# GpSimd adds the two states of a group before TensorE transposes their sum

## The reference

```
h = da * h + dbu              # da = exp(dt * A), dbu = dt * B * u
y = einsum('bdn,bn->bd', h, c)
y = (y + u * D) * silu(z);  out = y @ W_out
```

## Time and profile before

| | |
|---|---|
| Median of 3 runs | 1932.57 (1929.4 to 1938.46) |
| Profiled execution, its own time | 1930.86 |
| Its span, first to last instruction | 1928.9 |
| PE (TensorE matmul) busy | 1582.0 (82%) |
| DVE (VectorE) busy | 1511.5 (78%) |
| ACT (ScalarE) busy | 1004.7 (52%) |
| POOL (GpSimd) busy | 829.6 (43%) |
| Mean granted TensorE clock | 0.88 of full speed |

### The profile page before, as it was taken

The page is one execution under the profiler, slowest core; times in us unless marked ns, Lnnn a source line. Parts: engine busy times, 40 slices in busy tenths (PEclk is TensorE's granted clock), DMA queues, the critical chain, the costliest instruction groups (busy, mean ns, idle before and its releaser), DMA issues. The chain is left out here.

```text
span 1928.9 us, 16561 instructions
## 1 busy us (share of the span) xinstructions
PE 1582.0 (82%) x5776; PEld 834.9 (43%) x5776; DVE 1511.5 (78%) x1622; ACT 1004.7 (52%) x1609; POOL 829.6 (43%) x443
## 2 busy tenths in 40 slices
PE   6767877788888779988788879988798988886975
PEld 2445334443456335543355335453355434552433
DVE  4896789957996889968998789969899689963242
ACT  4542755346663755537563655637554565633522
POOL 0764265515553265515554166524555155630000
PEclk9767888797899889997999879997999879997987
DMA  4000000000000000000000000000000000000000
GB/s 155 1 1 11 13 0 1 11 13 0 1 1 11 13 11 1 1 23 0 11 0 11 12 11 0 0 22 1 11 0 11 12 0 11 0 11 0 11 0 22
DMA packets 18058, 20.51 MB, mean 11 GB/s; under 512 B 1361, under 2 KB 16977, under 8 KB 18017
## 3 DMA queue, kind: packets, MB, share of 16 engines
q1 hardware_dynamic: 18016, 19.98, 3.2%
HBM read 15.79 MB, written 4.19 MB: 10 GB/s over the span
## 5 line engine op out<-in xcount | busy, mean ns | idle before, releaser
L419 POOL TENSOR_TENSOR reg_a<-reg_a,cb 128x1024 f32<-128x1024 f32 x256 | 603.5, 2358 | 476.3 <-DVE reg_a L1116 476.3
L1116 DVE TENSOR_TENSOR_SCAN reg_a<-reg_a,pb 128x1024 f32<-128x1024 f32 x256 | 584.2, 2282 | 30.4 <-ACT reg_a L884 19.9
L884 ACT ACTIVATE reg_a<-dt,neg_a 128x511 f32<-128x511 f32 x512 | 336.8, 709 | 46.7 <-DVE reg_a L1116 46.5
L1106 DVE TENSOR_TENSOR pb<-pb,dtu 128x1024 f32<-128x1024 f32 x256 | 309.8, 1210 | 65.4 <-PE pb L617 53.4
L638 PE MATMUL py<-ident,reg_a 128*128 128x128 f32 x2048 | 304.4, 298 | 22.8 <-POOL reg_a L419 22.8
L638 PEld LDWEIGHTS py<-ident,reg_a 128*128 128x128 f32 x2048 | 273.3, 156 | 76.1 <-POOL reg_a L419 26.0
L617 PE MATMUL pb<-bcs,sel 96*128 96x512 bf16 x512 | 180.2, 440 | 95.1 <-DVE reg_a L1116 87.9
L519 PE MATMUL px<-hT,whh 128*128 128x512 f32 x384 | 203.7, 656 | 0.0
L786 ACT ACTIVATE xs<-px,half_b 128x512 f32<-128x512 f32 x96 | 66.0, 688 | 151.4 <-PE px L523 150.6
L617 PEld LDWEIGHTS pb<-bcs,sel 96*128 96x128 bf16 x512 | 38.2, 103 | 245.0 <-DVE reg_a L1116 146.9
L596 PE MATMUL pc<-x2T,w_fc 128*128 128x512 f32 x224 | 110.0, 615 | 20.9 <-DVE reg_y L1130 13.5
(11 more groups left out here) (179 smaller groups left out, 2318.4 us busy)
## 6 DMA issues: line engine op xcount, KB each, us to landing
xin<-x_in SPq DMA_DIRECT2D x9, 512.0 KB, 3.6
xs<-x_in SPq DMA_DIRECT2D x8, 512.0 KB, 3.4
x_out<-reg_m SPq DMA_DIRECT2D x8, 512.0 KB, 3.0
w_in<-w_inT_in SPq DMA_DIRECT2D x1, 1024.0 KB, 6.4
w_fc<-w_fcT_in SPq DMA_DIRECT2D x1, 1024.0 KB, 10.7
w_pr<-w_prT_in SPq DMA_DIRECT2D x1, 1024.0 KB, 13.0
xs<-wihT_in SPq DMA_DIRECT2D x1, 768.0 KB, 8.6
whh<-whhT_in SPq DMA_DIRECT2D x1, 768.0 KB, 8.7
```

What stands on the lines that cost most here:

```text
L419: pool.tensor_tensor(h[:, g % HR], h[:, g % HR], cb[:, 2 * q:2 * q + 2], ALU.mult).then_inc(s["hc_done"], 1)
L884: ins = act.activation(d_a[:, g % 2, j, 1:], dt[:, c, 1:], ACT.Exp, scale=neg_a[:, c * NS + n + j:c * NS + n + j + 1])
L1106: dve.tensor_tensor(pb[:, b:b + 2, :], pb[:, b:b + 2, :], dtu[:, c:c + 1, :].to_broadcast([P, 2, L]), ALU.mult).then_inc(s["mul_done"], 1)
L1116: dve.tensor_tensor_scan(h2[:, g % HR], d_a2[:, g % 2], pb[:, b:b + 2, :].rearrange("p a t -> p (a t)"), 0.0, ALU.mult, ALU.add).then_inc( ...
```

## The change

GpSimd gets a second instruction per group. After the multiply with C it waits for its own completion and adds state 1 of the slot to state 0, in place, 128x512; the new semaphore `hp_done` signals it. TensorE waits for `hp_done` in place of `hc_done` and transposes only the four blocks of state 0, which now hold the sum of both. The accumulation in `py` runs over the 8 groups of a chunk.

```diff
@@ -81,7 +81,7 @@
-cb_full cb_ready bcb_full da_ready mul_done scan_done hc_done hsum_done ypost_done yz_done
+cb_full cb_ready bcb_full da_ready mul_done scan_done hc_done hp_done hsum_done ypost_done yz_done
@@ -417,6 +417,8 @@
                         pool.tensor_tensor(h[:, g % HR], h[:, g % HR], cb[:, 2 * q:2 * q + 2], ALU.mult).then_inc(s["hc_done"], 1)
+                        pool.wait_ge(s["hc_done"], g + 1)
+                        pool.tensor_tensor(h[:, g % HR, 0], h[:, g % HR, 0], h[:, g % HR, 1], ALU.add).then_inc(s["hp_done"], 1)
                     if mamba and chunk_end(g) is not None:
@@ -629,14 +631,13 @@
                 c, q = g // PAIRS, g % PAIRS
-                pe.wait_ge(s["hc_done"], g + 1)
+                pe.wait_ge(s["hp_done"], g + 1)
                 if q == 0 and c:
                     pe.wait_ge(s["yt_ready"], c)
-                for j in range(2):
-                    for i2 in range(TT):
-                        cols_ = slice(i2 * P, (i2 + 1) * P)
-                        mm = pe.matmul(py[:, cols_], h[:, g % HR, j, cols_], ident[:], is_transpose=True,
-                                       start=(q == 0 and j == 0 and i2 == 0), stop=(q == PAIRS - 1 and j == 1), skip_group_check=True)
+                for i2 in range(TT):
+                    cols_ = slice(i2 * P, (i2 + 1) * P)
+                    mm = pe.matmul(py[:, cols_], h[:, g % HR, 0, cols_], ident[:], is_transpose=True,
+                                   start=(q == 0 and i2 == 0), stop=(q == PAIRS - 1), skip_group_check=True)
                 mm.then_inc(s["hsum_done"], 1)
```

## The result

The changed kernel takes 2006.72 us (median of 4 runs, 2002.22 to 2010.7) against 1931.92 for the kernel before: ratio 1.0388, 95% interval 1.0369 to 1.0406. It is slower by 75 us where 34 were forecast; the stated range ended at 1986. The sign was right, the size off by a factor of two.

What follows compares the result with a forecast made beforehand. VectorE was taken as the bound, with 15 us idle per batch. Seven full batches at +3.5 (3.6 + 3.6 + 2.4 + 0.9 - 7.0) gave +24.5, with pass 0 +34: 1965 us from 1930.9, range 1938 to 1986.

Steps and rivals of the forecast that it cites:

- The collisions on VectorE: Full passes: adds delay VectorE's SBUF-to-SBUF instructions L1014/L1016, L1027/L1029 and L1019 by 3.6, 3.6 and 2.4 us per pass.
- Taking turns on the port: VectorE's SBUF-to-SBUF instructions and GpSimd's alternate, each waiting for the other's to finish; an add costs the second instruction 1.2 us.
- rival 3: GpSimd keeps the port through multiply and add, or TensorE is granted less clock: 4 us more per batch, 1993; chance 0.15.
- The gains on TensorE's side: Full passes: fewer transposes shorten VectorE's idle time behind TensorE by 2.2, 3.0 and 1.75 us in three rounds, together 7.0.
- The prediction's own sign: Full batch: VectorE's idle time for the broadcasts of B (L617) falls from 6.8 us to under 3.
- Its part on the clock: Whole kernel: granted clock may shift either way, +-20 us at the extreme; taken as zero.
- Pass 0: First batch: GpSimd becomes the bound at 3.66 us per group; +9.5 us, bounds +6 and +13.
- the drought: Pass 0, merge of the weights: GpSimd runs out of work while TensorE is away from the groups; 1.5 us.
- The end of a pass: After a batch's last scan nothing covers GpSimd: +1.32 us for the add, -0.43 for fewer transposes, +0.9.
- Rival 1: TensorE was the hidden bound and L1016 and L1029 escape collisions: full batch gains 6.1 us, 1897; chance 0.12.
- Rival 2: A wash: collisions about 5 us per batch in place of 9.6, about 1933; chance 0.15.
- rival 4: The add doesn't bind in pass 0: 9.5 us less, 1955; chance counted within the forecast's 0.58.

Runs made afterwards that it cites:

- The run with memsets: Changed kernel with three waiting GpSimd memsets of a scratch tile, together about 1.3 us, in place of each add; state 1 left out of y: 1964.7 us, ratio 1.0154.
- a choice by groups: Changed kernel with add and four transposes only in ten groups of passes 1 to 7, eight transposes elsewhere: 1910.4 us, ratio 0.9894 to the kernel before.
- the kernel with twenty adds: Changed kernel with add and four transposes only in 20 of 32 groups of passes 1 to 7, none in pass 0: 1934.3 us, ratio 1.0009.

## Why the prediction was wrong in size

- *The collisions on VectorE* (3.6 + 3.6 + 2.4 = 9.6 per full pass, 67): the mechanism was right, the sum right partly by luck. VectorE's busy time rose by 70.1. But the two pairs brought 17 and 20 in place of 25 each: the second instruction waits 0.95 (medians 1.64 and 2.17) in place of 1.2, and six of the 24 L1017 and three of the 24 L1030 met no add (three rounds of each lie in the pass without a Mamba block). L1020 brought 20 for 17. L937, which was set to be hidden, made up for the shortfall with 11 us. The run with memsets adds what the prediction had only for L1019: half of the 70 comes from a late GpSimd, not from the add's own reading.
- *Taking turns on the port*: right: the exclusive port pair of the Trainium skill's "SBUF — State Buffer" ("SBUF: two separate sides") holds in the timeline of L1015 and L1017, and only instructions with SBUF operands alone were held here. So rival 3 (GpSimd keeps the port) is out in its first form: L1028 is unchanged (2945 to 2939 ns), L1009 no longer than before (median 1.50 in both). The other half of rival 3, less clock, is what happened; its sign, a clock in the groups under 0.92, came (0.88).
- *The gains on TensorE's side* (7.0 per pass, 49): this is the step that failed. With the ends of the passes and pass 0 the prediction's terms for the removed transposes come to 53. Measured: 24 with the transposes removed only in the stretches for which the 49 were counted, 17 with all removed, 9.5 with all removed beside the add. So there are three shortfalls. First, even in those stretches a full pass gains 3.7, not 7.0: VectorE's waits for L617 and L790 shrink by 5.1 (in pass 4), but L1019 and L1050 then meet GpSimd, and the output projection comes 1.6 later by the clock. Pass 1, for which the same 7.0 was counted, gains nothing there. Second, the prediction took removals elsewhere for neutral. In the full passes they are; in pass 1 they cost 5.7, where TensorE comes to a stretch that binds at half clock. Third, beside the add another 8 go, which no run takes apart. The prediction's own sign, VectorE's wait for L617 falling from 6.8 to under 3 in a full pass, did not come (4.0 in pass 4 of the changed kernel, and 56.0 for 53.4 over the run). Its part on the clock took it for luck with two signs and set it to zero. Wherever transposes were removed in all groups or in those where nobody waits, the clock fell (0.846, 0.837, 0.861 for 0.880); removed only where VectorE waits, it stayed (0.883). No run changes the clock and nothing else, so what it costs is read from equal matmuls that took longer.
- *Pass 0* (+9.5): +12.6, and 13 to 15 by the run without the add there. GpSimd is the bound as forecast, its last transposes came at 184.35 for 182 (180.6 and the drought); the difference is the merge of the weights at half clock, with a VectorE wait of 6.92 for 4.36 and a drought of 3.5 for 1.5. But the pace of 3.66 held only for a few groups: after the merge the scans stand at 3.50, since the merge had emptied GpSimd's queue, and GpSimd fell behind again by 0.16 a group until the end.
- *The end of a pass* (+0.9): about +1.3, since four transposes at half clock take what eight took: nothing came off the 1.3 of the add.
- *The sum.* By the run with the add and eight transposes, the add costs 84, where the prediction's terms for it come to 87 (67 on VectorE, 7 x 1.3 at the ends, 10.5 in pass 0); the removed transposes give back 9.5, where they come to 53. So 87 - 53 = 34 was forecast and 84 - 9.5 = 75 measured: nearly the whole error is the gain on TensorE's side.
- Rival 1 (TensorE the hidden bound, the collisions missing) is refuted twice: the collisions came, and not over 24 us were to be had on TensorE's side. Rival 2 (collisions of 5 per batch) and rival 4 (the add hidden in pass 0) are out by the 70 and the 12.6.

## What to carry to other kernels

Removed work counts only where others wait for it, and not in full even there: behind the wait that shrinks stands the next one, here GpSimd's instructions and TensorE's clock. And on TensorE work removed where nobody waits can cost clock in the stretch behind it, as in pass 1. So take work off TensorE where it binds and leave it elsewhere: here removals in 16 of 32 groups gave 24 us, in all groups 17. Before GpSimd gets a second instruction, look for VectorE's instructions with SBUF operands only, in particular two in a row, and for those that come when GpSimd is late; they, and not GpSimd's mean load of 43%, decide, and a choice by groups turned 75 us of loss into 21 of gain. What each half of such a change is worth can be tested alone: one run with the new instruction and the old work, one with the removed work and no new instruction.

## What the runs showed that I had not expected

- Removing 448 of the 2048 transposes, and nothing else, cost 4.6 us (1936.4 for 1931.8), at a mean granted clock of 0.861 for 0.880. The loss is in the one pass without the feed-forward block beside Mamba and attention; in the full passes of the profiled execution it is nil.
- Plain matmuls with the identity and transposes that take as long hold the clock equally: 0.868 and 0.864 at 2016.7 and 2016.2 us.
- A 128x4 instruction of VectorE (L937) that reads SBUF alone, 0.17 when free, took up to 2.17 beside GpSimd.
- The same code took 1921.6 us at a clock of 0.872 and 1930.3 to 1936.5 at 0.853 to 0.859 (the kernel with twenty adds).
